# Expert part of a mixture-of-experts layer by token chunks of 512, with the experts' weights as the stationary operand

## The reference

```
x1 = x + layernorm(attention)           # 2048 x 256
xn = layernorm(x1)
probs = softmax(xn @ Wr)                # 8 experts; the two largest are kept and
combine = top2(probs) / their sum       # rescaled; zero for the other six
h[e] = silu(xn @ Wg[e]) * (xn @ Wu[e])  # every expert for every token, 176 wide
out = sum_e combine[e] * (h[e] @ Wd[e])
return x1 + layernorm(out)
```

## Time and profile before

| | us |
|---|---|
| median of 3 runs | 2849.79 (2846.68 to 2852.78) |
| span of the profiled execution (its only own time on the page; 7.6 below the median) | 2842.2 |
| PE busy | 2669.4 (94%) |
| PE weight loads busy | 2263.8 (80%) |
| DVE busy | 1978.3 (70%) |
| ACT busy | 1445.4 (51%) |
| POOL busy | 282.8 (10%) |

### The profile page before, as it was taken

One profiled execution on the slowest core, in us unless ns is written; L12 is line 12 of the kernel. 1 busy time (PEld: TensorE's weight loads), 2 busy tenths in 40 slices (PEclk: granted clock), 3 DMA queues, 4 the chain that ended last, 5 costly groups with the idle time before them and its releaser, 6 DMA issues.

```text
span 2842.2 us, 47075 instructions
## 1 busy us (share of the span) xinstructions
PE 2669.4 (94%) x15264; PEld 2263.8 (80%) x15264; DVE 1978.3 (70%) x3648; ACT 1445.4 (51%) x3035; POOL 282.8 (10%) x346
## 2 busy tenths in 40 slices
PE   4999999999999999999999999999999999949996
PEld 4788888888888888888888888888888788749995
DVE  4677767676767677777767676767677777755556
ACT  2555645464656555555556464646455555513332
POOL 1101010100101010101010100101010100030210
PEclk8999999999999999999999999999999999959998
DMA  5000000000000000000000000000000000020000
GB/s 104 8 5 12 5 13 5 6 11 2 16 2 16 2 15 2 13 5 13 5 13 5 12 6 2 16 2 16 2 16 1 6 1 1 1 61 9 24 0 30
DMA packets 52834, 34.22 MB, mean 12 GB/s; under 512 B 10040, under 2 KB 52408, under 8 KB 52408
## 3 DMA queue, kind: packets, MB, share of 16 engines
q1 hardware_dynamic: 52536, 30.59, 4.3%
HBM read 28.47 MB, written 2.10 MB: 11 GB/s over the span
## 4 chain that ended last, share of the span: by engine, by line
PE 89%; DVE 5%; issue 2%; DMA 1%; ACT 1%; SPq 1%; POOL 0%; DVEq 0%; ACTq 0%; POOLq 0%
PE ps_t L438 15%; PE ps_a L353 14%; PE ps_a L355 13%; PE ps_a L354 13%; PE ps_s L353 11%; PE ps_s L355 11%; PE ps_s L354 11%; DVE part_max L769 2%; DVE pT_lo L789 1%; PE ps_t L569 1%; DMA acc<-in_L_attn_bo 1%; ACT probs L619 1%; DVE xn L743 0%; POOL x L321 0%; DVE stats L730 0%
## 5 line engine op out<-in xcount | busy, mean ns | idle before, releaser
L628 ACT ACTIVATE pT_hi<-ps_t 128x512 fp32r<-128x512 f32 x1024 | 612.0, 598 | 767.8 <-PE ps_t L438 752.5
L789 DVE TENSOR_TENSOR pT_lo<-ps_t,pT_hi 128x512 fp32r<-128x512 f32 x1024 | 705.1, 689 | 325.9 <-ACT pT_hi L628 305.3
L619 ACT ACTIVATE probs<-ps_s,shift 128x512 f32<-128x512 f32 (+1 forms) x768 | 636.7, 829 | 303.0 <-DVE shift L783 303.0
L769 DVE TENSOR_REDUCE part_max<-ps_s 128x1 f32<-128x512 f32 (+1 forms) x768 | 662.9, 865 | 150.2 <-PE ps_s L355 140.7
L438 PEld LDWEIGHTS ps_t<-ident,probs 128*128 128x128 f32 x4096 | 511.2, 141 | 140.7 <-issue 8.3
L438 PE MATMUL ps_t<-ident,probs 128*128 128x128 f32 x4096 | 617.7, 274 | 0.8 <-ACT probs L619 0.8
L353 PE MATMUL ps_s<-kT_hi,qT_hi 128*128 128x512 f32 x1024 | 472.2, 461 | 45.1 <-issue 24.2
L353 PE MATMUL ps_a<-pT_hi,v_hi 128*128 128x512 f32 x1024 | 432.9, 423 | 34.0 <-DVE pT_lo L789 33.9
L355 PE MATMUL ps_s<-kT_hi,qT_lo 128*128 128x512 f32 x1024 | 411.1, 401 | 0.0
L354 PE MATMUL ps_s<-kT_lo,qT_hi 128*128 128x512 f32 x1024 | 409.8, 400 | 0.0
L355 PE MATMUL ps_a<-pT_hi,v_lo 128*128 128x512 f32 x1024 | 404.8, 395 | 0.0
(11 more groups left out here) (125 smaller groups left out, 3350.2 us busy)
## 6 DMA issues: line engine op xcount, KB each, us to landing
probs<-in_L_attn_x SPq DMA_DIRECT2D x4, 512.0 KB, 5.6
codes_k<-in_L_attn_wk_codes SPq DMA_DIRECT2D x16, 128.0 KB, 2.2
scales_k<-in_L_attn_wk_scales SPq DMA_DIRECT2D x64, 32.0 KB, 3.0
codes_q<-in_L_attn_wq_codes SPq DMA_DIRECT2D x16, 128.0 KB, 2.1
scales_q<-in_L_attn_wq_scales SPq DMA_DIRECT2D x64, 32.0 KB, 3.0
codes_v<-in_L_attn_wv_codes SPq DMA_DIRECT2D x16, 128.0 KB, 3.1
scales_v<-in_L_attn_wv_scales SPq DMA_DIRECT2D x64, 32.0 KB, 3.1
codes_o<-in_L_attn_wo_codes SPq DMA_DIRECT2D x16, 128.0 KB, 2.0
```

Source lines behind the costliest of these rows:

```text
L619: nc.scalar.activation(probs[:, j % 2, r, cols], ps_s[:, cols], ACT.Exp, bias=shift[:, j % 2, r:r + 1], scale=SCALE, accum_out=sums[:, j % ...
L628: nc.scalar.activation(pT_hi[:, k % RING, :], ps_t[:, k % 2, :], ACT.Copy).then_inc(sm["pt_hi"], 1)
L769: V.tensor_reduce(part_max[:, j % 2, r, part:part + 1], ps_s[:, slice(*MAX_PARTS[part])], AX.X, ALU.max)\
L789: V.tensor_tensor(pT_lo[:, k % RING, :], ps_t[:, k % 2, :], full(pT_hi[:, k % RING, :]), ALU.subtract)\
```

## The change

The attention stays. Behind it the work is ordered by chunks of 512 tokens (4 of them), and in a chunk by 11 groups of 128 hidden rows that run across the experts' borders: 44 steps.

- In a step PE makes gate and up apart, each 6 matmuls of 512 columns with the *weights* stationary and the transposed tokens moving, so the hidden values come out already transposed and `turn_hidden` falls away. The two results lie in two of four PSUM banks.
- The router's weight differs along the moving tokens and the stationary rows, so it can no longer be a scalar per partition. PE expands it: one matmul of 512 columns per step (`expand_comb`) of a 0/1 matrix `pick` (64 rows deep, 1408 columns, set up once by POOL, its lower half copied by DVE) with the transposed `comb`. DVE multiplies twice per step.
- `down` takes the hidden values as stationary operand, 12 matmuls of 256 columns per step, two steps later (`LAG`), and all 11 groups add up in PSUM; the add into `y` falls away. ACT copies the sum out once per chunk.
- h_lo is made by POOL; the weights' high parts are split by ACT and the low parts by POOL, group by group, in the first chunk's steps.
- The norms, transposes, logits and ranking of chunk c+1 (`pre`) and the norm, residual and store of chunk c-1 (`post`) are put behind the steps of chunk c by two tables. Only chunk 0's `pre` runs before the first step. The final add moves from DVE to POOL.
- `x` and three of four weight pieces are loaded in the attention's last chunk, `Wr` and the last piece behind it. The result goes out in 8 DMAs of 256 KB.

```diff
+        PRE_AT = ["", "", "", "", "std", "turn0", "turn1", "logits", "rank", "turn_comb", ""]
+        POST_AT = ["", "copy", "stats0", "stats1", "std", "out", "", "", "", "", ""]
...
+            sp.wait_ge(sm["t_ready"], KT * (CHUNKS - 1))
+            load_gate_up(0)
...
-                    last = product3(ps_s[:, b * CH:b * CH + 2 * I], xT_hi[:, c, rows], xT_lo[:, c, rows],
-                                    gu_hi[:, u, c, :], gu_lo[:, u, c, :], first=c == 0, last=c == DC - 1)
...
+                for w, free, ready in ((0, "silu_done", "gate_ready"), (1, "mul_done", "up_ready")):
+                    wait(pe, free, n - 1)
+                    bank = 2 * (n % 2) + w
+                    for cc in range(DC):
+                        last = product3(ps_s[:, bank * CH:(bank + 1) * CH], gu_hi[:, cc, w, cols], gu_lo[:, cc, w, cols],
+                                        xT_hi[:, cc, rows], xT_lo[:, cc, rows], first=cc == 0, last=cc == DC - 1)
+                    last.then_inc(sm[ready], 1)
...
+                wait(pe, "hid_done", n)
+                nc.tensor.matmul(ps_comb, pick[:, g * P:(g + 1) * P], combT[:, c % 2, :], start=True, stop=True)\
+                    .then_inc(sm["comb_x"], 1)
...
+                pe.wait_ge(sm["h_lo_done"], n + 1)
...
-            experts(pe, pair)
+            pre_all(pe, pre)
+            for n in range(STEPS + LAG):
+                if n < STEPS:
+                    gate_up(n)
+                    expand_comb(n)
+                if n >= LAG:
+                    down(n - LAG)
+                hooks(n, pre, post)
...
+            def gates(n):
+                act.wait_ge(sm["gate_ready"], n + 1)
+                wait(act, "mul_done", n - 1)
...
+            def hidden_hi(n):
+                act.wait_ge(sm["hid_done"], n + 1)
+                wait(act, "down_done", n - HRING + 1)
...
+            dve.wait_ge(sm["pick_hi_done"], 1)
+            V.tensor_copy(pick[EP:2 * EP, :], pick[0:EP, :]).then_inc(sm["pick_done"], 1)
```

More of the change, by code:

```diff
@@ L176, in has, with pre_all, hooks @@
             return not isinstance(h, int) or 0 <= h * NCH + j + ahead < CHUNKS
+        PRE_AT = ["", "", "", "", "std", "turn0", "turn1", "logits", "rank", "turn_comb", ""]
+        POST_AT = ["", "copy", "stats0", "stats1", "std", "out", "", "", "", "", ""]
+        def pre_all(eng, pre, split=None):
+            for s in range(G):
+                pre(0, s)
+                if split is not None and s in (0, 4):
+                    split(s // 4)
+        def hooks(n, pre, post):
+            c, s = n // G, n % G
+            if 0 < c:
+                if c < NCH:
+                    post(c - 1, s)
+                elif s:
+                    for last in range(s, G):
+                        post(c - 1, last)
+            if c + 1 < NCH:
+                pre(c + 1, s)
         @block.sync
@@ L238, in _ @@
[L238 to L244, removed]
+            load_gate_up(3)
             ov = out[0].rearrange("(t p) d -> p t d", p=P)
-            for t in range(0, TT, 4):
-                sp.wait_ge(sm["out_ready"], t + 4)
-                sp.dma_start(ov[:, t:t + 4, :], xn2[:, t:t + 4, :]).then_inc(sm["out_stored"], 16)
@@ L318, in residual @@
[L318 to L346, removed]
+            pool.wait_ge(sm["out_lo"], CHUNKS)
+            pool.memset(combT[:, :, :].bitcast(f32), 0.0).then_inc(sm["combT_zero"], 1)
+            pool.memset(before[:, :, :], 1.0).then_inc(sm["pick_set"], 1)
+            pool.memset(full(pick[:, :]), 1.0).then_inc(sm["pick_set"], 1)
@@ L535, in _ @@
             heads(pe, body)
[L538 to L546, removed]
@@ L564, in turn_hidden @@
[L564 to L580, removed]
@@ new lines, in expand_comb, with down @@
+            def expand_comb(n):
+                c, g = n // G, n % G
+                if n == 0:
+                    pe.wait_ge(sm["pick_done"], 1)
+                if g == 0:
+                    pe.wait_ge(sm["combT_lo"], c + 1)
+                wait(pe, "hid_done", n)
+                nc.tensor.matmul(ps_comb, pick[:, g * P:(g + 1) * P], combT[:, c % 2, :], start=True, stop=True)\
+                    .then_inc(sm["comb_x"], 1)
+            def down(n):
+                c, g = n // G, n % G
+                if c == 0:
+                    pe.wait_ge(sm["d_lo_done"], g + 1)
+                pe.wait_ge(sm["h_lo_done"], n + 1)
+                if g == 0:
+                    wait(pe, "y_copied", 2 * c)
+                for a in range(TPC):
+                    rows = slice(a * P, (a + 1) * P)
+                    dst = ps_a[:, a // 2, (a % 2) * D:(a % 2 + 1) * D]
+                    hi, lo, end = h_hi[:, n % HRING, rows], h_lo[:, n % HRING, rows], g == G - 1
+                    nc.tensor.matmul(dst, hi, d_hi[:, g, :], start=g == 0 and a % 2 == 0, stop=False,
+                                     skip_group_check=True)
+                    nc.tensor.matmul(dst, hi, d_lo[:, g, :], start=False, stop=False, skip_group_check=True)
+                    last = nc.tensor.matmul(dst, lo, d_hi[:, g, :], start=False, stop=end, skip_group_check=True)
+                last.then_inc(sm["down_done"], 1)
@@ L722, in _ @@
+            act.wait_ge(sm["acc_done"], 2 * CHUNKS)
+            act.wait_ge(sm["out_lo"], CHUNKS)
+            pre_all(act, pre, split_hi)
+            for n in range(STEPS + LAG):
+                if n < STEPS:
+                    gates(n)
+                if 1 <= n <= STEPS:
+                    hidden_hi(n - 1)
+                if n + 2 < G:
+                    split_hi(n + 2)
+                hooks(n, pre, post)
         @block.vector
@@ L988 @@
+            pre_all(dve, pre)
+            for n in range(STEPS + LAG):
+                if n < STEPS:
+                    hidden(n)
+                hooks(n, pre, post)
 _INS = ["x", "wq_codes", "wq_scales", "bq", "wk_codes", "wk_scales", "bk", "wv_codes", "wv_scales", "bv",
```

465 lines of the change are left out of this document (289 added, 176 removed).

## The result

| | before | after |
|---|---|---|
| median (4 runs each) | 2850.69 (2846.68 to 2852.78) | 2775.7 (2775.19 to 2775.99) |
| span of the profiled execution | 2842.2 | 2773.3 |
| its own time | not on its page | 2775.19 |
| attention's last accumulation | 2493.4 | 2505.4 |
| from there to the end of the span | 348.8 | 267.9 |

The ratio is 0.9738 (95% interval 0.9724 to 0.9752): 75 us faster, where I had said 93 (2757 us). The direction and the range held. What was wrong is the size: I forecast 18.7 us too little time.

What follows compares the result with a forecast made beforehand. PE bound the expert loop. Behind the attention, opening 33.1, steps 194, hooks 12, waits 2, clock 3, last low part 1 and end 10.7 make 255.8 for 348.8: span 2749.2, plus 7.6 offset, 2757 us; range 2747 to 2779.

Steps and rivals of the forecast that it cites:

- Each matmul still brings its own weight load … hidden at 0.230: Expert loop: weight loads stay hidden behind 512-column matmuls at 0.230 us each; the 64-row expansion's depth switch taken as 0.
- leave the first 2493.4 us as they are: Attention: same instructions and no DMA conflict, so its 2493.4 us of the span stay unchanged.
- The loop by columns: Expert loop: 13 matmuls at 0.230 and 12 at 0.118 make 4.41 us a step, 194 for 44 steps.
- Hooks on PE: Between the loop's steps: `pre`'s transposes and logits on PE paid in full, 4.1 us a chunk, 12 for three.
- Waits at the fifth steps: Fifth step of the two middle chunks: PE waits for `xn2_done` behind DVE's roots and norms, 2 us in all.
- The clock: Loop's start: the clock stays at half speed for 5.8 us after the dense stream begins, costing 3 us.
- Rival 2: Logits between the loop's steps: they bring the clock down in each of three chunks, some 17 us, 2774; chance 0.10.
- Rival 3: Whole loop: waits between groups keep the clock at 0.50, 206 us more, 2963 if all of it; chance 0.02.
- The opening: From the attention's end to the first step: `pick` set-up and copy, then chunk 0's `pre`; 33.1 us, bounds 28 and 41.
- The rule on the shared port: DVE beside POOL: they block each other at the shared SBUF port; 2.3 us of the opening, 1.3 root, 1.0 norms.
- The end: Behind the last step's `down`: copy, statistics, root, norm, four POOL adds and the last DMA; 10.7 us, before 25.7.
- Rival 1: First chunk and steps with a root or ranking: DVE, POOL and ACT interlock more than counted, 18 us, 2775; chance 0.16.

Runs made afterwards that it cites:

- e1: Changed kernel with `pick` and `combT` given 128 rows instead of 64, the new rows multiplying by zero, so the expanding matmul is 128 deep; 2754.65 us.
- e2: Changed kernel with the 64-row expanding matmul issued twice in a row with the same operands; 2782.18 us.
- e3: Changed kernel without the expanding matmul and DVE's second multiplication, so experts are summed unweighted; 2745.05 us.
- e4: The kernel before, unchanged, profiled again; 2847.3 us, span 2845.5.
- e5: Changed kernel with all four chunks' `pre` placed before the first step and `combT` in four slots; 2826.47 us.
- e6: Changed kernel with GpSimd making the low part of the hidden values twice in every step; 2776.42 us.
- e8: 128-row-expansion kernel (e1) with `pick` set up behind chunk 0's residual adds and norms, its copy and the router weights' split moved later; 2748.76 us.
- e9: Changed kernel with 128 rows in the expansion, the loop over heads written out and the set-up of `pick` moved, all together; 2701.96 us.
- e10: The kernel before with its loop over heads written out, nothing else; 2799.58 us.
- e7: Changed kernel with the loop over heads 1 to 14 written out on all engines; 2720.84 us.

## Why the prediction came out as it did

Against 2756.8, which I rounded to 2757, the median is 18.9 us more: 12.1 behind the attention (267.9 for 255.8), 12.0 in it, and 5.2 less outside, since the offset of 7.6 became 2.4 from the span to the median (1.9 in the profiled execution itself). Behind the attention the parts are the opening 3.1 less, the loop 16 more and the end 0.8 less.

- **Failed: "Each matmul still brings its own weight load … hidden at 0.230"**, and with it the expansion's depth. I bounded the switch by 0 to 0.1 us and took 0, "since rows of full depth are the nearest". It is 0.39 us a step, 17 us (e1, e2, e3). The bound came from the start of a matmul behind a group of transposes, which is a different place: there the depth goes from 128 to 88 rows and not to 64, and only on the way in. I also had named the price a second time, as 0.3 us a step, and called it "small here". The Trainium skill has the rule, in "TensorEngine Tiling (Array Packing)", section "Tiling Modes": a change of tiling mode drains TensorE. I did not weigh it. The traces agree, by PE's weight loads, which stand idle 0.37 and 0.24 us at the two changes and are early on either side of them.
- **Failed: "leave the first 2493.4 us as they are".** The instructions were the same, the time was not: 7.6 us between the span and the median was no constant around the program, but the luck of one execution: in e4 the distance is 1.8. I had two numbers that didn't fit, a span below every timed run by 4.5 us, and called it an offset.
- The loop by columns: 0.24 and 0.12 a matmul, 4.455 us a step with full depth (e1) for 4.41. Right to 1%; 2 us of 44 steps.
- Hooks on PE: 3.9 us per chunk, 12 in all. Right. Having them there hides 58 us (e5).
- Waits at the fifth steps: 2 us predicted, none came; the steps were longer. Where slack shrinks they appear, with 0.2 us in each middle chunk in e1 and 0.3 to 0.4 in e6.
- The clock: it rose 2.3 us behind the first dense matmul, not 5.8, and cost 1.2 instead of 3; but it fell once at the logits (1.6). Rival 2 had the right place and a price too high: not 17 us but 1.6 per fall. Rival 3 did not come: the loop ran at 0.99.
- The opening: 30.0 for 33.1. The selects were 1.35 and 1.40 us (I took 2.0), the copy 0.88 (1.2). The set-up ended 5.4 us behind the attention (7.1); DVE did wait for it, 1.25 us.
- The rule on the shared port held: four norms took 2.81 against 1.38 us (e1, e8). It was worth 1.4 us at the norms, where I had counted 1.0, and 0.4 at the root's addition (0.53 against 0.17), where I had counted 1.3. It was also worth 0.75 at the cast of the router's weights, which I had not counted.
- The end: 9.9 for 10.7; the wait for the last low part 0.3 for 1.

Rival 1's number (2775) is the measured one, but not its mechanism: no wait of PE is listed in the changed kernel's loop, and the opening was shorter than forecast. Its sum was wrong besides: 1 us in nine steps and 3 in three are already the 18, and the opening's upper end would have added 8. A time alone would have confirmed the wrong cause. That the range held is in part luck too: of the two errors that fill it, the attention's 12 us belongs to no rival that I had named.

## What to carry to other kernels

Where matmuls of 64 rows and of 128 alternate, look at the weight loads and not only at the columns: a load that is not pulled ahead costs on the way in and on the way out, and zero rows up to the common depth were free here. From 88 to 128 rows the trace of before shows no such cost. Before predicting from one profiled execution, compare it with the timed runs and look at the granted clock in the part that the change leaves alone, and add experiments up by stretches, not by medians. An "issue" wait at a loop's turn deserves a trial with the loop written out: here a gap of 2 us a turn, 1.6 of which came back, and more again by the clock behind it.

## What the runs showed of the hardware that I had not expected

- An expansion of 64 rows between matmuls of 128 costs 0.63 us, one of 128 rows 0.24. The change from 88 to 128 rows in the kernel before shows no cost.
- The turn of the loop over heads leaves 1.6 to 2.1 us without a matmul, and the clock is at 0.50 for 0, 3.4 or 6.8 us from there on. Without the loop 56 us of 2505 are gone in the changed kernel, 45 of 2493 in the kernel before, and the spread of the kernel before falls from 8 us (nine runs beside e9 and e10) or 15 (seven beside e1 to e4) to 2 (four of e10).
- Behind 24 matmuls of 8 columns (2.66 us, with no gap in the dense stream) the clock falls in some chunks: in one of three in the profile after and in e6, in two in e1, e3, e7 and e8, in all three in e2 and e9. Which it will be, none of the runs settles.
